# Fixed places for the sorted tokens of each expert, sends spread over the attention stretches, and nine output sums added straight from PSUM

## The reference

```
logits = x @ router                      # [B, S, 8]
weights, indices = top_k(softmax(logits), 2);  norm_weights = softmax(weights)
out = sum over the two chosen e of norm_weight[e] * ((silu(x @ gate[e]) * (x @ up[e])) @ down[e])
x = x + layernorm(out)
```

## Time and profile before

| | us |
|---|---|
| median of 3 runs (1507.39 to 1509.79) | 1509.08 |
| the profiled execution: its own time | 1509.86 |
| its span in the trace | 1507.8 |
| PE busy, DVE busy, ACT busy, POOL busy | 1399.6, 1171.5, 1066.0, 1218.0 |

### The profile page before, as it was taken

The page is one execution under the profiler, slowest core; times in us unless marked ns, Lnnn a source line. Parts: engine busy times, 40 slices in busy tenths (PEclk is TensorE's granted clock), DMA queues, the critical chain, the costliest instruction groups (busy, mean ns, idle before and its releaser), DMA issues. The chain is left out here.

```text
span 1507.8 us, 45164 instructions
## 1 busy us (share of the span) xinstructions
PE 1399.6 (93%) x17865; PEld 930.0 (62%) x17865; DVE 1171.5 (78%) x2689; ACT 1066.0 (71%) x2072; POOL 1218.0 (81%) x730
## 2 busy tenths in 40 slices
PE   4899999999999999999999999999999898869995
PEld 1366665666666656666665656666666555659994
DVE  7788887777788788887788788777887888845576
ACT  2677787778877877778788777777877665724344
POOL 5588998888888988989889889899789878825374
PEclk7799999999999999999999999999999999979998
DMA  5444443423232223333333333233232242133222
GB/s 172 116 110 114 114 110 89 110 72 78 65 89 82 72 77 102 79 79 79 90 81 86 79 79 92 75 83 80 76 82 72 58 160 66 46 119 98 68 58 73
DMA packets 101488, 132.87 MB, mean 88 GB/s; under 512 B 16672, under 2 KB 51232, under 8 KB 100896
## 3 DMA queue, kind: packets, MB, share of 16 engines
q1 hardware_dynamic: 98208, 123.70, 30.8%
q0 software_dynamic: 3072, 6.30, 1.5%
HBM read 20.49 MB, written 14.94 MB: 23 GB/s over the span
## 5 line engine op out<-in xcount | busy, mean ns | idle before, releaser
L1200 ACT ACTIVATE probs<-psum 128x512 f32<-128x512 f32 x1024 | 615.1, 604 | 190.7 <-PE psum L913 189.6
L1946 POOL TENSOR_TENSOR probs_lo<-probs 128x1024 f16<-128x1024 f32 x301 | 626.2, 2090 | 113.6 <-ACT probs L1200 112.2
L1494 DVE CUSTOM_DVE_ANT_0 scan_out<-psum,ahead 128x512 f16<-128x512 f32 x512 | 349.4, 686 | 198.1 <-PE psum L808 189.1
L932 PE MATMUL psum<-cv,probs 128*128 128x66 f16 x4096 | 476.8, 193 | 13.3 <-POOL probs_lo L1946 12.8
L934 PE MATMUL psum<-cv,probs 128*128 128x64 f16 x4096 | 476.5, 194 | 0.0
L936 PE MATMUL psum<-cv,probs_lo 128*128 128x66 f16 x4096 | 475.2, 192 | 0.0
L934 PEld LDWEIGHTS psum<-cv,probs 128*128 128x128 bf16 x4096 | 380.6, 97 | 110.7 <-issue 3.1
L932 PEld LDWEIGHTS psum<-cv,probs 128*128 128x128 bf16 x4096 | 385.7, 97 | 74.8 <-POOL probs_lo L1946 12.1
L911 PE MATMUL psum<-q_both,k_twice 128*128 128x512 f16 x1024 | 388.4, 379 | 2.8 <-ACT probs L1200 2.8
L913 PE MATMUL psum<-q_max,k_ones 65*128 65x512 f16 x1024 | 390.9, 382 | 0.0
L936 PEld LDWEIGHTS psum<-cv,probs_lo 128*128 128x128 f16 x4096 | 380.3, 98 | 0.0
(11 more groups left out here) (219 smaller groups left out, 1898.8 us busy)
## 6 DMA issues: line engine op xcount, KB each, us to landing
t_swapped<-t_sin SPq DMA_DIRECT2D x248, 128.0 KB, 2.0
k_twice<-qk_hi SPq DMA_DIRECT2D x128, 128.0 KB, 2.4
q_lone<-qk_hi SPq DMA_DIRECT2D x64, 128.0 KB, 2.3
q_both<-qk_hi SPq DMA_DIRECT2D x64, 128.0 KB, 2.3
q_both<-qk_lo SPq DMA_DIRECT2D x64, 128.0 KB, 2.4
q_max<-qk_hi SPq DMA_DIRECT2D x64, 128.0 KB, 2.3
k_ones<-qk_lo SPq DMA_DIRECT2D x64, 128.0 KB, 2.4
z_unit<-slots_in SPq DMA_DIRECT2D x31, 128.0 KB, 2.5
```

Source lines behind the costliest of these rows:

```text
L932: pe.matmul(acc, high[:, q * P:(q + 1) * P, 1], v[:, 0:VLO], start=opens, stop=False, skip_group_check=True)
L1200: act.activation(probs[s % 4][:, i, :], score_ps[tile % SCORE_BANKS], ACT.Exp, scale=SCALE).then_inc(probs_done, 1)
L1494: dve.tensor_tensor_reduce(scan_out[m % 2][:], bank[BANK_OF["base", n, m]], ahead[m % 2][:], 1.0, LOWEST, ALU.add, ALU.max, max_all[a][:, ...
L1946: pool.tensor_tensor(probs_lo[s % 4][:].rearrange("p a n -> p (a n)"), p, p.bitcast(BF16).rearrange("p (n two) -> p n two", two=2)[:, :, 1 ...
```

## The change

- **Places.** Each expert gets room for the most rows it can have (12 units of 256), in one tensor `slots` of 26,368 rows, which is used for the inputs and, in place, for the outputs. A token's slot is then expert * 3072 + rank, which is known when its own batch is ranked: the base is added on PE by one more matmul in `rank_tokens`, and `take_ranks` writes `slot_of` itself. Units past the last full one have room behind.
- **Place.** `place` now makes the list of the units' first rows (`row_of`) and of their experts. It moves from step 1 to step 15 of stretch 29. Ranks move from step 15 of stretches 12, 20, 28 to step 1 of 13, 21, 29. SP reads the first rows from SBUF into registers, four at a time, for loads and stores.
- **Sends.** Batch 0's 16 sends and batch 1's 16 sends stand in steps 3, 5 and 7 of stretches 14 to 28 (3, 3, 1, 1, 3, 0, 2, 3, 3, 3, 2, 2, 3, 0, 3 of them). Batch 2's 16 sends stand at the odd steps of stretches 30 and 31. Each waits for `ranked` (at the first of a batch) and for the exponents of the step before.
- **Clearing** is 26 DMAs instead of 8, four in a stretch, in stretches 1 to 7.
- **Output sums.** For the nine pairs m in `DIRECT`, DVE adds the PSUM bank to `oacc` at steps 7 and 9 of stretch m+1; ACT's copy and POOL's sum are gone for these.
- **Low halves.** Stretch 29 goes back to the usual six DVE steps; 30 has eight, 31 twelve for DVE.
- **Gathers.** Each of the 48 gathers waits for a unit in turn (`fuse_done` or `added`), two for each dense unit from the third on.

```diff
+SLOTS = E * MOST_UNITS * UNIT
+ALL_SLOTS = SLOTS + (SORTED - CHOICES * MOST_UNITS) * UNIT
...
-LATE_DVE_STEPS = {GROUPS - 3: (2, 4, 6, 8, 10, 13, 15), GROUPS - 2: (0, 1, 2, 3, 5, 6, 7, 8, 9, 11, 12, 13, 14, 15),
-                  GROUPS - 1: tuple(range(STEPS))}
+LATE_DVE_STEPS = {GROUPS - 2: (1, 3, 5, 7, 9, 11, 13, 15), GROUPS - 1: (0, 1, 2, 4, 5, 6, 8, 9, 10, 12, 13, 14)}
...
-RANK_AT, PLACE_AT = (4, 15), (5, 1)
+RANK_AT, PLACE_AT = (5, 1), (5, 15)
...
-SEND_AT = ([(LAST - 2, s) for s in (11, 12, 13, 14, 15, 15)]
-           + [(LAST - 1, s) for s in range(STEPS) for _ in range(2 if s % 3 == 0 and s else 1)]
-           + [(LAST, s) for s in range(14) for _ in range(1 + s % 2)])
+SEND_AT = [(g, s) for g, steps in ((14, (3, 5, 7)), (15, (3, 5, 7)), (16, (7,)), (17, (7,)), (18, (3, 5, 7)), (20, (5, 7)),
+                                   (21, (3, 5, 7)), (22, (3, 5, 7)), (23, (3, 5, 7)), (24, (3, 7)), (25, (3, 7)),
+                                   (26, (3, 5, 7)), (28, (3, 5, 7)), (30, range(1, STEPS, 2)), (31, range(1, STEPS, 2))) for s in steps]
 assert len(SEND_AT) == len(SENT)
+FIRST_GATHER = 2
+
+DIRECT = (13, 14, 17, 19, 20, 21, 22, 25, 27)
...
-        to_clear = [(at, min(clear_rows, SORTED * UNIT - at)) for at in range(0, SORTED * UNIT, clear_rows)]
+        to_clear = [(at, min(clear_rows, ALL_SLOTS - at)) for at in range(0, ALL_SLOTS, clear_rows)]
...
+            def clear_slots(g, i):
+                if not 0 < g < PAIRS or 4 * (g - 1) + i >= len(to_clear):
+                    return
+                at, n = to_clear[4 * (g - 1) + i]
+                sp.dma_start(slots[at:at + n, :].rearrange("(p r) d -> p (r d)", p=P),
+                             oacc[1][:, 0:n * D // P]).then_inc(cleared, 16)
...
+            def first_row(unit, regs):
+                if unit % IDS_AT_ONCE == 0:
+                    sp.wait_ge(placed, 1)
+                    sp.load(regs, row_of[0:1, unit:unit + IDS_AT_ONCE])
+                return sp.snap(regs[unit % IDS_AT_ONCE], min_val=0, max_val=ALL_SLOTS - UNIT)
...
             def load_unit(unit):
+                first = first_row(unit, rows_from)
                 if unit >= SLOTS_IN:
                     sp.wait_ge(unit_turned, unit - SLOTS_IN + 1)
-                sp.dma_start(z_unit[unit % SLOTS_IN][:], unit_rows(slots_in, unit)).then_inc(unit_in[unit % SLOTS_IN], 16)
+                sp.dma_start(z_unit[unit % SLOTS_IN][:].bitcast(F32), unit_rows(first)).then_inc(unit_in[unit % SLOTS_IN], 16)
 
             def store_unit(unit):
+                first = first_row(unit, rows_to)
                 sp.wait_ge(y_done, unit + 1)
-                sp.dma_start(unit_rows(slots_out, unit), y_sb[unit % ROWS_OUT][:]).then_inc(y_out[unit % ROWS_OUT], 16)
+                sp.dma_start(unit_rows(first), y_sb[unit % ROWS_OUT][:]).then_inc(y_out[unit % ROWS_OUT], 16)
...
+            def add_projected(m, c):
+                dve.wait_ge(out_ready, 4 * m + (c + 3))
+                if m - 1 in DIRECT:
+                    dve.wait_ge(out_copied, 2 * (m - 1) + (c + 1))
+                else:
+                    dve.wait_ge(out_added, added_by(m - 1, c))
+                total = oacc[batch_of(m) % 2][:, c * HALF:(c + 1) * HALF]
+                dve.tensor_tensor(total, total, bank[BANK_OF["out", m, c]], ALU.add).then_inc(out_copied, 1)
...
                 dve.wait_ge(rank_ready, n + 1)
                 src = job_bank("rank", n, 0)
                 before = src[:, 0:TILES * E].rearrange("p (t e) -> p t e", e=E)
                 for k in range(CHOICES):
                     last = dve.tensor_tensor(rank_parts[:, k], before, hots[:, n, k], ALU.mult)
-                dve.tensor_copy(counts[:], src[:, TILES * E:TILES * E + E]).then_inc(rank_steps, 1)
-                dve.wait_ge(rank_steps, n + 1)
+                step(dve.tensor_copy(counts[:], src[:, TILES * E:TILES * E + E]), 1)
                 standing()
-                dve.tensor_reduce(ranks[:, n], rank_parts[:], AX, ALU.add).then_inc(ranked, 1)
+                with nc.allow_low_precision(reason="one of eight parts is not zero, and it is a whole number"):
+                    dve.tensor_reduce(slot_of[:, n], rank_parts[:], AX, ALU.add).then_inc(ranked, 1)
...
                 step(dve.tensor_reduce(units_of[:], over_step[:], AX, ALU.add), 2)
+                dve.tensor_scalar(unused[:], units_of[0:1, :], -float(UNIT), float(MOST_UNITS * UNIT), ALU.mult, ALU.add)
                 step(dve.tensor_tensor_scan(unit_ends[:], units_of[:], zeros[:], 0.0, ALU.add, ALU.add), 3)
-                step(dve.tensor_tensor(slot_base[:], unit_ends[:], units_of[:], ALU.subtract), 4)
-                step(dve.tensor_scalar(slot_base[:], slot_base[:], float(UNIT), None, ALU.mult), 5)
-                own = hots[:, 0:EARLY].rearrange("p b k t e -> p (b k t) e")
-                dve.tensor_tensor(past[:], unit_at[:].unsqueeze(2).to_broadcast([1, COLUMNS, E]),
-                                  unit_ends[0:1, :].unsqueeze(1).to_broadcast([1, COLUMNS, E]), ALU.is_ge)
-                step(dve.tensor_tensor(base_parts[:, 0:rows], own, slot_base[:].unsqueeze(1).to_broadcast([P, rows, E]), ALU.mult), 6)
-                dve.tensor_reduce(expert_of[:], past[:], AX, ALU.add)
-                step(dve.tensor_reduce(base_sum[:, 0:rows], base_parts[:, 0:rows], AX, ALU.add), 7)
-                step(dve.tensor_scalar(column_of[:], expert_of[:], float(E - 1), float(F), ALU.min,
-                                       ALU.mult), 8)
-                to = slot_of[:, 0:EARLY].rearrange("p b k t -> p (b k t)")
-                step(dve.tensor_tensor(to, base_sum[:, 0:rows], ranks[:, 0:EARLY].rearrange("p b k t -> p (b k t)"),
-                                       ALU.add), 9)
+                step(dve.tensor_tensor(past[:], unit_at[:].unsqueeze(2).to_broadcast([1, COLUMNS, E]),
+                                       unit_ends[0:1, :].unsqueeze(1).to_broadcast([1, COLUMNS, E]), ALU.is_ge), 4)
+                dve.tensor_tensor(jumps[:], past[:], unused[:].unsqueeze(1).to_broadcast([1, COLUMNS, E]), ALU.mult)
+                step(dve.tensor_reduce(expert_of[:], past[:], AX, ALU.add), 5)
+                step(dve.tensor_reduce(jump[:], jumps[:], AX, ALU.add), 6)
+                dve.tensor_scalar(column_of[:], expert_of[:], float(E - 1), float(F), ALU.min, ALU.mult)
+                step(dve.tensor_tensor(row_of[:], jump[:], steps_of[0:1, :], ALU.add), 7)
...
+                here = [sent_row for sent_row, at in zip(SENT, SEND_AT) if at == (g, s)]
+                for i, (n, t, k) in enumerate(here):
                     if (t, k) == (0, 0):
-                        pool.wait_ge(placed, 1)
+                        pool.wait_ge(ranked, n + 1)
                         pool.wait_ge(z_lo_done, CHUNKS * (n + 1))
+                    if 2 * s + i:
+                        pool.wait_ge(probs_done, g * KEY_TILES + 2 * s + i)
                     send(n, t, k)
...
+                beside = FIRST_GATHER + made // 2
+                if made % 2 == 0:
+                    pool.wait_ge(fuse_done, SORTED + beside + 1)
+                else:
+                    pool.wait_ge(added, beside - DOWN_LAG + 1)
```

More of the change, by code:

```diff
@@ L260, in sem @@
             return ctx.enter_context(nc.semaphore(name))
-        slots_in = nc.dram_tensor("slots_in", (SORTED * UNIT, 2 * D), F16, kind="Internal").ap()
+        slots = nc.dram_tensor("slots", (ALL_SLOTS, D), F32, kind="Internal").ap()
         clear_rows = 4 * UNIT
-        slots_out = nc.dram_tensor("slots_out", (SORTED * UNIT, D), F32, kind="Internal").ap()
         x1_kept = nc.dram_tensor("x1_kept", (EARLY, P, TILES * D), F32, kind="Internal").ap()
@@ L330, in program @@
         rank_parts = sb("rank_parts", [P, CHOICES, TILES, E])
-        ranks = sb("ranks", [P, B, CHOICES, TILES])
+        base_rows = sb("base_rows", [P, TILES * E], F16)
         counts = sb("counts", [P, E])
-        steps_of = sb("steps_of", [P, MOST_UNITS])
+        steps_of = sb("steps_of", [P, COLUMNS])
         over_step = sb("over_step", [P, E, MOST_UNITS])
@@ L542, in outputs_added, with added_by @@
         def outputs_added(b):
-            return CHUNKS * PAIRS * (b + 1)
+            return added_by(PAIRS * (b + 1) - 1, CHUNKS - 1)
+        def added_by(m, c):
+            assert m not in DIRECT
+            return CHUNKS * (m - sum(d < m for d in DIRECT)) + (c + 1)
         def tile_range(half):
@@ L550, in in_dram, with unit_rows @@
             return t[bass.ds(b, 1)].rearrange("b (t p) d -> p (b t) d", p=P)
-        def unit_rows(rows, unit):
-            return rows[unit * UNIT:(unit + 1) * UNIT, :].rearrange("(i p) d -> p i d", p=P)
+        def unit_rows(first):
+            return slots[bass.ds(first, UNIT), :].rearrange("(i p) d -> p i d", p=P)
         def dense(unit):
@@ L688, in _ @@
                         sp.wait_ge(clear_set, 1)
-                    for piece in to_clear[2 * (r - 1):2 * r]:
-                        clear_slots(*piece)
```

(14 more changed lines are left out.)

37 lines of the change are left out of this document (19 added, 18 removed).

## The result

The changed kernel takes 1533.13 us (median of 4 runs, 1530.18 to 1540.09), the kernel before 1509.02 (4 runs, 1507.39 to 1509.79): ratio 1.0175, 95% interval 1.0159 to 1.0191. It is slower; I had forecast 1487, range 1477 to 1501. The profiled execution took 1533.12, its span is 1531.3.

What follows compares the result with a forecast made beforehand. PE was taken to bound attention except late, where POOL's 48 sends set its end, and PE again afterwards. Terms 12.4 + 14.3 + 0.9 - 1.0 - 3.0 - 0.5 - 0.5 = 22.6 us saved from 1509.86; forecast 1487, range 1477 to 1501.

Steps and rivals of the forecast that it cites:

- Stretches 12 to 28: Attention stretches with early sends, direct sums and moved ranks: 3.0 us lost, 2.0 for sends and sums, 1.0 for ranks.
- sends and sums: Stretches 12 to 28: POOL's added sends less its fewer sums mostly hidden; 2.0 us lost, bounds -3 and +12.
- Rival (a): Stretches 14 to 28: POOL becomes the bound, late `rope_add` holds ACT's exponents, PE starves; 32.4 if nothing hidden, 1517; chance 0.06.
- rival (b): Late stretches keep their excess through exchange of locks and place, 12 to 28 lose 4 more: 1499; chance 0.19.
- The page against the change: Early sends beside DVE's low halves: by the skill's port-lock rule they would cost 75 us, not 55.
- Ranks: Stretches 13, 21 and 29: PE stalls 1.8 us for the ranks' bank; 0.5 us each taken as lost.
- Stretches 29 and 30: 77.5 us against 89.90, 12.4 saved, bounds 8 and 15; includes a 2.0 us stall from place, falling into 30.
- Stretch 31 and the hole: Stretch 31 loses 1.0 us; PE's pause before the expert units saves 14.3, its slow restart 0.9.
- Clearing, gathers, rest: More clearing DMAs lose 0.5 us, gather waits in the expert phase 0.5; the rest costs nothing.
- 14 to 18 and 20 to 26 each within 1 us: Sign the forecast is right: these attention stretches each stay within 1 us of their length before.
- No stretch over 41 us after 28: Sign the forecast is right: no stretch after stretch 28 takes over 41 us.
- the wait of over 2 us at steps 0 to 2 of stretch 30: Sign the forecast is wrong: PE waits over 2 us at steps 0 to 2 of stretch 30.

Runs made afterwards that it cites:

- the two added waits: Changed kernel, all sends kept, POOL made to wait in stretches 14 to 28 for DVE's `k_diff` and step-8 low half: 1508.37 us beside 1507.93 before.

## Why the prediction was wrong, by its steps

- **Stretches 12 to 28: the step that failed.** Predicted 3.0 lost (sends and sums 2.0, bounds -3 and +12), measured nothing in 12 and 13 together and 41.0 in 14 to 28. The term that failed is the one for sends and sums, and with it the overlap that it rests on. I set POOL's extra work (2.6 us a stretch) against POOL's idle time (5.9) and called it hidden. The idle time did hide the work; but DVE's instructions with two SBUF inputs had got through in those gaps, and without them PE waited for the maxima (26.2 us instead of 1.9) and ran at a lower clock. I had the row for it, a low half of 3.35 us beside one of POOL, and used it only for stretch 31, as "up to 1.90" each. The upper bound of 12 was the sums' bound and held nothing for this, and neither did the 32.4 of the rival, the price of POOL's work: sends cost 37.8.
- **Rival (a)** had the side and nearly the point from which it decides (1.9 us a stretch; measured 3 to 4), at 1517, but by `rope_add` and ACT. POOL kept idle time and ACT's exponents waited for no `rope_add`. No rival had DVE's two-input instructions as its mechanism for these stretches; rival (b) had it for the late ones.
- **The page against the change.** Sends do get longer (median 1.78 against 1.43). In the changed kernel 41 of the 48 have a DVE instruction with two SBUF inputs beside them, median 1.78; the other seven take 0.97 to 1.01. The Trainium skill ("SBUF — State Buffer", "SBUF: two separate sides") tells the trap for operations of VectorE in a 2-port mode; here it is seen beside its TENSOR_TENSOR. But this wasn't the harm: the two added waits left the sends where they were and took 30 us away. The same section has the lock work the other way too: of a VectorE operation with two SBUF inputs and a GpSimd operation that reads SBUF, the one that starts first gets the ports for its whole instruction and the other is blocked. That half I left out of these stretches, and the runs agree that it is the one that cost. "Held for a whole instruction" is still too little for what they show: 8.20 and 6.70 us cover several POOL instructions.
- **Ranks.** The stall of 1.64 came as worked out (1.8), in stretch 21 and 29; I booked 0.5 against the wait at step 15 that goes. Stretch 21 lost 4.0, a second wait of 1.87 among it. It kept this loss without sends (42.15) and went back to 38.3 in the versions with ranks in step 15, which also took a direct sum out of it; with only the direct sums taken back it took 39.9.
- **Stretches 29 and 30.** Predicted 77.5, measured 82.1: 7.8 saved, not 12.4. Stretch 30 was better than said (34.93, PE full), the stall of place, by the cut of the windows, fell into 29 and was 5.5, not 2.0, and place took 7.3 us and not 5.
- **Stretch 31 and the hole.** Predicted 14.2 in all (14.3 + 0.9 - 1.0), measured 11.8. The last send starts at 1349.22, the units' loads at 1352.25, and PE waits 1.14 us for them at 1354.61: as predicted. The 2.4 short go with PE's waits for low halves in 31, 4.0 us in four places, against 1.0 booked; three of the four are for DVE's.
- **Clearing, gathers, rest.** Predicted 1.0 lost, measured nothing up to stretch 10 and 1.1 in the expert phase: the size is right. Which part of the 1.1 is the gathers' isn't shown; `weigh` of the last ones waits 0.29 as against 0.27.

Of the signs named beforehand, "14 to 18 and 20 to 26 each within 1 us" failed, and rightly told where to look. "No stretch over 41 us after 28" failed as well (29: 47.15), and the wait of over 2 us at steps 0 to 2 of stretch 30 came: the 5.52 stands just before PE turns the attention of step 1 of that stretch.

## What to carry to other kernels

Idle time of POOL isn't free where DVE works beside it on SBUF: before filling it, list the DVE instructions with SBUF inputs that start in that stretch and ask whether POOL will still pause before each. What counts is where POOL's gapless runs of tensor instructions fall, not its load; two waits that make POOL pause while the critical DVE instructions run gave back 30 us, nearly as much as all the moving of sends, ranks and sums (32). And a row in which an instruction takes three times its usual length is a mechanism to price everywhere it can recur.

## What the hardware showed that I had not expected

- DVE instructions with a PSUM input kept their time beside POOL's runs (scan 0.68, sum from PSUM 0.67 to 0.68). Those with two SBUF inputs that met a POOL instruction waited for its end or, having missed that, for POOL's next gap, whatever their size: `k_diff` took 2.3, 6.47 or 7.87 for 0.95, a low half 8.20 for 1.22, the 128-column comparison 6.70. A small TENSOR_SCALAR took 1.45, a TENSOR_REDUCE beside the same run kept its 0.25.
- A POOL DMA issue makes such a gap: sends split POOL's run, and a held instruction got in just before one of them (POOL pauses for 0.16 us before the send at 1057.64 in stretch 25 of the run with two waits, where a low half took 6.37).
- The same kernel took 1508 and 1565 us at different times, on one and the same chip. The excess lies in the expert phase, in waits that the profile puts down to "remote". Of the kernel before, in that condition:

```profile
PE psum L1041 <- DVE y_got L1783: 39.7, 7, 22.8
ACT act_sb L1291 <- remote: 32.2, 4, 21.9
DVE y_got L1783 <- remote: 23.4, 4, 12.6
```

The gathers run at that time without pause, and of the instruction queue one packet moved in 30 us. That instruction loads stand behind the gathers there is a guess; no run tested it, since the version without pacing ran only when nothing stalled.
